# Layer two of a two-layer attention block: four self-attentions in a row, then four cross-attentions, instead of an interleaved order

## The reference, cut to what matters

```python
# layer 1: halves x0, x1 (1024 tokens each), adaLN modulation, then
x0 += gate * mha(mod(ln(x0)));  x1 += gate * mha(mod(ln(x1)))       # self-attention per half
x0 += gate * attend(q(x0), k(x1), v(x1)) @ proj;  x1 likewise       # each half attends to the other
x  += gate * gelu(mod(ln(x)) @ fc1) @ fc2
# layer 2:
x = layernorm(x + mha(x, x, x, mask))            # self-attention; in the fast branch all valid keys are 512
x = layernorm(x + mha(x, ctx, ctx, None))        # cross-attention over 1601 context tokens
x = layernorm(x + relu(x @ w1 + b1) @ w2 + b2)
```

## Time and profile before

| | us |
|---|---|
| median of 3 executions (lowest, highest) | 2359.86 (2359.76, 2363.3) |
| profiled execution, its own time | 2357.39 |
| span of its rows | 2355.5 |
| busy in it: PE / DVE / ACT / POOL | 2062.8 / 1564.8 / 1286.9 / 472.5 |
| mean granted TensorE clock | 0.921 of full |

### The profile page before, as it was taken

How to read it: one execution, slowest core, us unless ns; L and a number is a source line. 1 busy time by engine, 2 the same in 40 slices (tenths; PEclk the granted TensorE clock), 3 DMA queues, 4 the chain that set the end, 5 groups by cost and what they waited for, 6 DMA issues and landing times. The chain is left out here.

```text
span 2355.5 us, 33848 instructions
## 1 busy us (share of the span) xinstructions
PE 2062.8 (88%) x12890; PEld 808.0 (34%) x12890; DVE 1564.8 (66%) x2867; ACT 1286.9 (55%) x2406; POOL 472.5 (20%) x464
## 2 busy tenths in 40 slices
PE   4788988998888899989898897899798998999975
PEld 2422222322233252433433442332243334434324
DVE  3486977786776748457465656686657995796703
ACT  1035766565445577655674562568334784685660
POOL 0024333424132210114022332120103102102100
PEclk9678999998799899899999996999789999999987
DMA  6624313333034202034013621200202020000000
GB/s 147 125 71 101 98 51 78 99 74 82 15 84 104 69 3 51 3 66 128 13 42 78 116 87 43 55 17 6 49 3 53 20 38 13 12 11 9 12 15 11
DMA packets 97305, 126.66 MB, mean 54 GB/s; under 512 B 25293, under 2 KB 81982, under 8 KB 92014
## 3 DMA queue, kind: packets, MB, share of 16 engines
q1 hardware_dynamic: 97134, 124.42, 22.5%
HBM read 89.95 MB, written 24.74 MB: 49 GB/s over the span
## 5 line engine op out<-in xcount | busy, mean ns | idle before, releaser
L1573 ACT ACTIVATE PT<-ps 128x512 f32<-128x512 f32 (+1 forms) x2112 | 1099.7, 602 | 782.6 <-PE ps L1358 776.3
L1642 DVE TENSOR_REDUCE mx<-ps 128x1 f32<-128x512 f32 x2048 | 1281.8, 682 | 275.0 <-PE ps L1379 271.9
L1379 PE MATMUL ps<-KS,QS 49*128 49x512 bf16 x2048 | 545.5, 405 | 136.2 <-DVE mx L1642 90.5
L1358 PE MATMUL ps<-QS,KS 51*128 51x512 bf16 (+3 forms) x4224 | 624.6, 392 | 19.3 <-DMA QS<-mr 18.9
L1405 PE MATMUL ps<-PT,Vt 128*32 128x512 f32 (+1 forms) x4224 | 585.9, 627 | 0.0
L1379 PEld LDWEIGHTS ps<-KS,QS 49*128 49x128 bf16 x2048 | 148.6, 95 | 735.9 <-DVE mx L1642 509.8
L1358 PEld LDWEIGHTS ps<-QS,KS 51*128 51x128 bf16 (+3 forms) x4224 | 210.4, 97 | 285.1 <-ACT PT L1573 82.7
L1882 POOL CAST nm<-nm 128x16 bf16<-128x16 f32 x64 | 12.7, 198 | 663.8 <-DVE nm L1655 663.8
L1405 PEld LDWEIGHTS ps<-PT,Vt 128*32 128x32 f32 (+1 forms) x4224 | 84.8, 109 | 152.9 <-issue 149.4
L1488 PE MATMUL ps<-wP,OD 128*128 128x256 f32 x256 | 79.1, 476 | 57.7 <-POOL OD L1915 34.8
L1500 PE MATMUL ps<-XT,big 128*128 128x256 f32 x512 | 125.8, 396 | 2.3 <-ACT big L1615 1.4
(11 more groups left out here) (106 smaller groups left out, 1120.7 us busy)
## 6 DMA issues: line engine op xcount, KB each, us to landing
scr<-S SPq DMA_DIRECT2D x28, 768.0 KB, 3.6
big<-in_mask_1x1xSxS_ik SPq DMA_DIRECT2D x16, 1024.0 KB, 5.8
QS<-scr SPq DMA_DIRECT2D x32, 384.0 KB, 8.5
KS<-scr SPq DMA_DIRECT2D x24, 384.0 KB, 8.2
QS<-scr SPq DMA_DIRECT2D x32, 256.0 KB, 4.7
ON<-Oe SPq DMA_DIRECT2D x256, 32.0 KB
OD<-scr_r SPq DMA_DIRECT2D x32, 256.0 KB
KS<-scr SPq DMA_DIRECT2D x24, 256.0 KB, 5.0
```

What stands on the lines that cost most here:

```text
L1358: z = eng.matmul(ps[0:w, it.bank[j], :], KS[lo:hi, part, pr, col:col + w], QS[lo:hi, part, u.qs, pr, :], start=part == 0, stop=part == 1 a ...
L1379: return eng.matmul(mbank(it)[:, 0:w], QS[lo:lo + MR, 0, u.qs, pr, 128 * it.tq:128 * it.tq + 128], KS[lo:lo + MR, 0, pr, it.lo:it.hi], sta ...
L1573: eng.activation(PT[0:w, it.pt * 4 + 2 * it.pp + j, :], ps[0:w, it.bank[j], :], ACT.Exp, scale=0.25).then_inc(S["exp_done"], 1)
L1642: eng.tensor_reduce(out=mx[:, u.b, c, it.i:it.i + 1], in_=mbank(it)[:, 0:it.hi - it.lo], axis=AX.X, op=ALU.max).then_inc(S["max_done"], 1)
```

## The change

The order table puts the self-attention of chunk 1 before the cross-attention of chunk 2. With it go the query buffers (chunk 1's self-attention now uses 1, chunk 2's cross-attention 0) and the due units of the background chains: the context chunks are due at 48 instead of 44, the MLP of layer 1 for chunk 1 at 43 instead of 47, and the ends of the self-attentions at 48, 52, 56, 60 instead of 44, 48, 52, 60. No operation of the computation is added or taken away. Two reloads of the Q weights and two of the output weights fall away, because the kind changes less often.

```diff
-                    work.post(44, ctx_kv(0, 512, 4, now()))
-                    work.post(44, ctx_kv(3, 512, 4, now()))
+                    work.post(48, ctx_kv(0, 512, 4, now()))
+                    work.post(48, ctx_kv(3, 512, 4, now()))
...
-                    work.post(44, ctx_kv(1, 512, 4, now()))
-                    work.post(44, ctx_kv(2, 512, 4, now()))
-                    work.post(44, [("sa2", lambda: None)] + x_q(2, 1, "ca"), 0)
-                    work.post(48, x_q(1, 0, "sa"))
+                    work.post(48, ctx_kv(1, 512, 4, now()))
+                    work.post(48, ctx_kv(2, 512, 4, now()))
+                    work.post(44, x_q(1, 1, "sa"))
+                    work.post(48, [("sa2", lambda: None)] + x_q(2, 0, "ca"))
...
-                    work.post(47, mlp0(1) + [(0, lambda: slow.append([6, l1_mlp_start]))])
+                    work.post(43, mlp0(1) + [(0, lambda: slow.append([6, l1_mlp_start]))])
...
-                end_l1({2: 44, 3: 48, 0: 52, 1: 60}[c], c, "sa")
+                end_l1({2: 48, 3: 52, 0: 56, 1: 60}[c], c, "sa")
...
-            order = [(p1, 2), (p1, 3), (p1, 0), (p1, 1), (p2, 2), (p2, 3), (p2, 0), (p3, 2),
-                     (p2, 1), (p3, 3), (p3, 0), (p3, 1)]
+            order = [(p1, 2), (p1, 3), (p1, 0), (p1, 1), (p2, 2), (p2, 3), (p2, 0), (p2, 1),
+                     (p3, 2), (p3, 3), (p3, 0), (p3, 1)]
```

## The result

| | before | after |
|---|---|---|
| median of 10 executions each, us | 2356.16 (2352.14 to 2363.3) | 2367.6 (2363.24 to 2372.61) |
| ratio of the two | 1 | 1.0044, 95% interval 1.0029 to 1.0058 |
| profiled execution's span | 2355.5 | 2361.4 |
| start of layer 2 (end of unit 31) to end of unit 63 | 1050.05 | 1062.93 |

The change made the kernel 0.44% slower, where I had forecast 0.2% faster. The profiled span grew by only 5.9 us, since layer 1, which is the same in both, happened to take 4.4 us less in that execution (unit 31 ends at 1226.22 and at 1221.81), and what follows unit 63 took 2.6 us less. Layer 2 alone grew by 12.9; I had written -5.2. So I compare units.

The account below looks back on a forecast made before the run. PE was taken to bound the cross-attention stretches, with low clock and waits in the short units. Terms 8 - 22 - 18 + 4.4 + 22.4 = -5.2 us gave 2354.7 from 2359.86; range 2341 to 2369.

Parts of the forecast that it names:

- Terms for units 40 to 55 (-22, -18, +4.4, +22.4): Changes in us for units 40-43, 44-47, 48-51 and 52-55, priced by like units in the trace.
- the surviving crossing: Short unit then long unit, left in self-attention of 1 (unit 46): priced like unit 42 before, 44.2 us.
- The second term: Units 44-47, self-attention of 1: 98.4 us against 116.4 in its old place, so -18.
- Term for units 32 to 39 (+8): Self-attention of 2 and 3: 180.8 us against 172.7, with the MLP first and a 10 us wait in unit 37.
- The waits before the output projections grow further: Rival: transfers ahead of scr_r<-dd on SP's queue in units 36 and 40 lengthen waits; 2362 to 2372 us, chance 0.20.
- The waits stay as they are: Rival: small transfer not held back, unit 37 waits 1 to 8 us, 41 waits 7.7; 2338 to 2348, chance 0.25.
- The clock stays low: Rival: granted clock stays low through the block of short units; about 2383 us, chance 0.05.
- The signs that I had named: One short unit over 40 us, 42 near 18, 53 at 66, waits 10, 10, 14, 10, PE busy 20 less.
- the three signs that the forecast is wrong: Unit 42 stays above 25 us, unit 37 has no wait, or stretch 52-55 is not 20 us longer.
- Four weight loads, which nothing waits for long: The only work that the reorder takes away, in layer 2; nothing was said to wait long for it.

Follow-up runs that it names:

- both orders with the better queue: Old and new order of attentions (new with contexts first), query loads issued behind the norm chain's load; ratios to the kernel before 0.9883 and 0.9749.

## Why the prediction was wrong

- **Terms for units 40 to 55 (-22, -18, +4.4, +22.4): near, one of them by luck.** Measured -20.8, -20.8, +5.4 and +24.5; together -11.7 where I had -13.2. Unit 42 went from 44.2 to 19.4 (I said 18.5), the surviving crossing 46 took 43.7 (44.2), unit 53 took 66.0 (66.0). The wait in unit 41 was 15.3 (14). The second term was luck in part. I had 11.5 for unit 44 and about 31 for unit 45; they took 20.6 and 19.5. PE waited 6.7 us for the maxima's load in unit 44, which stood behind the query loads, and by the time of the output projection in unit 45 the norm chain was ready, so that the wait of 10 us that I had there didn't come. (The four summands that I name for that stretch give 98.7 or 96.5, by which of the two like units is taken, and not 98.4.)
- **Term for units 32 to 39 (+8): wrong, +25.1.** This is the step that failed, and in it the assumption that a unit costs what a unit of the same content costs elsewhere, plus the wait before the output projection, on the one transfer of SP's queue that I followed. Three parts: unit 38, 27.0 for 14.4, from the maxima's load behind the keys' store and loads; unit 33, 33.2 for 27.4, from the statistics that I priced at 1 us; unit 36, 21.2 for 16.7, with 2.9 us of waiting for another QS<-mr. That is +12.6, +5.8 and +4.5. Against them unit 37 took 28.7 for 35: the norm chain was ready when I said (OD<-scr_r issued at 22.2 us after the end of unit 35; I had 22, though 3.9 + 9.1 + 8 + 2.7, my own numbers, make 23.7), but PE came later, at 25.7 instead of 20.4, so that it waited 4.0 and not 10. With the wait in unit 38 taken away, the kernel took 2352.9 us, near my forecast of 2354.7.
- **The rivals.** "The waits before the output projections grow further" had the right sign and, at 2362 to 2372, the range that the median of 2367.6 falls in, but for another reason: such waits grew by only 2.9 us behind POOL and by 4.5 in the row put down to issue, while those for QS<-mr grew by 19, of which it says nothing. "The waits stay as they are" had unit 37 right (1 to 8 us, measured 4.0) and unit 41 wrong (7.7, measured 15.3). "The clock stays low" had a part in it: unit 38 ran at 0.77 and unit 33 at 0.74, each with a wait of about 10 us in it; without the wait unit 38 was back at 1.00.
- **The signs that I had named.** One unit over 40 us instead of two, unit 42 near 18 (19.4, at a clock of 0.94), unit 53 at 66, some 20 us less of PE busy time (2062.8 to 2043.8), the waits in units 33 and 41 came; the waits of 10 us in units 37 and 45 did not. Of the three signs that the forecast is wrong, none did, and it was wrong. They all watched the places that I had thought about, and none the waits for QS<-mr.
- **The rule of the Trainium skill on completion order ("DMA: Bandwidth & Descriptors", "Queues, rings and completion order").** It leaves it open that the small transfer lands ahead of larger ones that were issued before it. Here it did not: it took 9.1 us to land behind the query loads and 3.0 ahead of them.
- **"Four weight loads, which nothing waits for long":** true of the kernel before. With the MLP first in the old order one of them held PE for 2.8 us in unit 40, so what they are worth hangs on what stands ahead of them in SP's queue.

One thing is left open: why unit 33's early statistics cost 6.6 us and not the 1.5 that DVE waits there for POOL. The trace shows PE busy 19.3 instead of 16.1 on the same 99 matmuls, at a granted clock of 0.74 instead of 0.81, and a wait of 2.8 us for DVE that the kernel before doesn't have; the rest was not taken apart.

## What to carry to other kernels

Price a reorder by units of the same content, but follow every transfer on the issuing queue, not only the large one that the argument is about: a load of 4 KB that stood behind a store, its landing and six loads held PE for 10 us, and with the clock that fell in the wait it cost at least as much as the kernel lost. When a reorder comes with new priorities for the background work, try the two apart; here the order was worth 1% and the priorities cost 1.3%. And where one in-order queue carries a chain of small transfers that an engine will wait for, issue the bulk loads that have slack behind it: in layer 2 that was worth 1.6%, more than the whole reorder; in layer 1, where PE's waits for that chain had been under 2 us, it was worth nothing.

## What the runs showed of the hardware

A DMA of 32 KB that was issued behind 1.57 MB on the same queue landed 9.1 us after its issue; with one load of 512 KB ahead of it, it took 3.0 us, and with no bulk load just ahead of it 1.45 us. Behind the query loads and the six key loads, in unit 40 of the changed kernel, it took 15.3 us.

TensorE's granted clock over a short unit that waits for the maxima of a long one was 0.58 to 0.64 in the kernels that were read for it (before, changed, and both orders with the better queue). Its 142 or 143 matmul records took 35.3 to 40.9 us, where the 99 records of a unit with the same projection but 16 maxima took 15.9 us at a clock of 1.00, 17.0 at 0.94 and 18.5 at 0.84.
